# Writing a head's scores in two goes, the second 0.3 slots after the first

## The reference

```python
x = layernorm(x)
q, k, v = proj(Wq, bq), proj(Wk, bk), proj(Wv, bv)          # 16 heads of 16
logits = einsum('bhqd,bhkd->bhqk', q, k) + einsum('bhqd,qkd->bhqk', q, rk)   # rk = embK[clip(k - q, -64, 64) + 64]
w = softmax(logits, axis=-1)
out = einsum('bhqk,bhkd->bhqd', w, v) + einsum('bhqk,qkd->bhqd', w, rv)
```

## Time and profile before

| | |
|---|---|
| median of three runs | 2844.34 us |
| the profiled execution's own time | 2847.89 us |
| its span, first to last instruction | 2846.1 us |
| TensorE busy | 2648.1 us, 93% |
| VectorE busy | 2036.7 us, 72% |
| ScalarE busy | 1573.9 us, 55% |
| GpSimd busy | 1018.2 us, 36% |
| mean granted TensorE clock | 0.983 of full speed |

### The profile page before, as it was taken

One profiled execution on the slowest core, in us unless ns is written; L12 is line 12 of the kernel. 1 busy time (PEld: TensorE's weight loads), 2 busy tenths in 40 slices (PEclk: granted clock), 3 DMA queues, 4 the chain that ended last, 5 costly groups with the idle time before them and its releaser, 6 DMA issues.

```text
span 2846.1 us, 102506 instructions
## 1 busy us (share of the span) xinstructions
PE 2648.1 (93%) x43218; PEld 1971.7 (69%) x43218; DVE 2036.7 (72%) x5187; ACT 1573.9 (55%) x2993; POOL 1018.2 (36%) x2275
## 2 busy tenths in 40 slices
PE   5899999999999999999999999999999999999995
PEld 3567777677776777667776777767777677777773
DVE  4776678676786677866787667776677766787774
ACT  3555556455555555555555565545665455565651
POOL 4113333433334333443234442334323433331025
PEclk8899999999999999999999999999999999999997
DMA  8545644446455464555545556446554456445410
GB/s 224 180 127 169 181 140 129 133 144 181 130 149 145 136 169 131 138 153 160 163 118 144 166 148 162 118 122 175 162 147 126 111 173 180 142 127 145 133 43 27
DMA packets 602999, 409.08 MB, mean 144 GB/s; under 512 B 145578, under 2 KB 602282, under 8 KB 602282
## 3 DMA queue, kind: packets, MB, share of 16 engines
q1 hardware_dynamic: 602538, 402.52, 50.1%
HBM read 206.83 MB, written 194.90 MB: 141 GB/s over the span
## 4 chain that ended last, share of the span: by engine, by line
PE 68%; DVE 16%; issue 5%; ACT 4%; POOL 3%; DMA 0%; SPq 0%; DVEq 0%; ACTq 0%; POOLq 0%
PE logitsT L755 14%; PE oacc L793 14%; PE scores L732 14%; PE logitsT L760 6%; DVE maxes L1012 6%; DVE junk L1009 5%; PE misc L856 4%; PE misc L692 4%; PE misc L818 3%; ACT wxr L1212 2%; PE misc L830 2%; PE misc L706 2%; PE misc L806 2%; POOL rs L1245 1%; DVE stats L915 1%
## 5 line engine op out<-in xcount | busy, mean ns | idle before, releaser
L1009 DVE CUSTOM_DVE_ANT_1 junk<-scores,bands 128x512 bf16<-128x512 f32 x988 | 680.2, 688 | 606.7 <-PE scores L732 588.5
L755 PE MATMUL logitsT<-qs,ks 98*128 98x128 bf16 (+3 forms) x9088 | 995.9, 216 | 33.6 <-ACT wxr L1212 24.6
L1212 ACT ACTIVATE wxr<-logitsT 128x512 f32<-128x512 f32 x1024 | 600.8, 602 | 584.6 <-PE logitsT L755 487.8
L755 PEld LDWEIGHTS logitsT<-qs,ks 98*128 98x128 bf16 (+1 forms) x9088 | 679.6, 99 | 272.4 <-issue 101.3
L1212 ACT ACTIVATE wy<-logitsT 128x512 f32<-128x512 f32 x1024 | 586.3, 596 | 432.1 <-PE logitsT L755 422.4
L732 PE MATMUL scores<-ks,qs 101*128 101x256 bf16 (+10 forms) x4096 | 719.3, 291 | 77.0 <-DVE maxes L1012 39.4
L1012 DVE TENSOR_REDUCE maxes<-scores 128x1 f32<-128x512 f32 x1024 | 701.6, 685 | 2.2 <-PE scores L732 2.2
L732 PEld LDWEIGHTS scores<-ks,qs 96*128 96x128 bf16 (+3 forms) x4096 | 299.7, 100 | 263.0 <-DVE maxes L1012 121.3
L760 PE MATMUL logitsT<-ident,bands 128*128 128x128 f32 x2048 | 468.5, 281 | 0.0
L1240 POOL TENSOR_SCALAR rs<-rs 128x1 int32<-128x1 int32 (+1 forms) x224 | 48.3, 216 | 977.8 <-DVE rs L920 975.3
L760 PEld LDWEIGHTS logitsT<-ident,bands 128*128 128x128 f32 x2048 | 292.7, 143 | 32.9
(11 more groups left out here) (136 smaller groups left out, 2678.8 us busy)
## 6 DMA issues: line engine op xcount, KB each, us to landing
bs<-praw SPq DMA_DIRECT2D x256, 512.0 KB, 4.2
bands<-bs SPq DMA_DIRECT2D x224, 512.0 KB, 4.4
ks<-kd SPq DMA_DIRECT2D x64, 384.0 KB, 4.9
qs<-qd SPq DMA_DIRECT2D x112, 192.0 KB
bands<-bs SPq DMA_DIRECT2D x128, 128.0 KB, 3.4
qd<-qparts SPq DMA_DIRECT2D x64, 192.0 KB, 2.8
kd<-kparts SPq DMA_DIRECT2D x64, 192.0 KB, 2.5
qd<-qparts SPq DMA_DIRECT2D x64, 128.0 KB, 2.6
```

Of the source, the lines that this page charges most:

```text
L755: mm = e.matmul(lt[:, c * P + q0:c * P + q1], kk[0:depth, h, kt * P:(kt + 1) * P], qs[i][0:depth, h, q0:q1], start=q0 == 0, stop=not near, ...
L1009: e.tensor_tensor_reduce(junk[:], scores[:, 0:512].rearrange("p (a c) -> p a c", a=2), banded, 1.0, LOWEST, ALU.add, ALU.max, mx[:, h, 0:1 ...
L1212: e.activation(dst, src, ACT.Exp).then_inc(exp_ready, 1)
```

## The change

The stage `row_max` of a head becomes two stages, `row_max` with half 0 and with half 1. The first keeps its slot, `m0 + 0.87 h`; the second is at `m0 + 0.87 h + 0.3`. On TensorE half 0 writes the first bank and half 1 the second; on VectorE half 0 is the custom instruction with the relative term, half 1 the plain reduction. Each of the two waits for what it waited for before: half 0 of head h+1 for VectorE's half 0 of head h, half 1 of head h+1 for VectorE's half 1 of head h. The instructions are the same in kind, shape and number. Stages whose slots fall between the two places now stand between the two halves, on TensorE and on VectorE. The lists of ScalarE, GpSimd and SyncE are the same as before.

```diff
--- before.py
+++ after.py
@@ -148,7 +148,8 @@
             at(r0 - 15 + 3.5 * blk, "band_write", s, blk)
             at(r0 - 9 + 4 * blk, "band_read", s, blk)
         for h in range(HG):
-            at(m0 + 0.87 * h, "row_max", s, h)
+            at(m0 + 0.87 * h, "row_max", s, h, 0)
+            at(m0 + 0.87 * h + 0.3, "row_max", s, h, 1)
         at(m0 + 6.4, "max_reduce", s)
         at(m0 + 7.4, "max_rows", s)
         at(m0 + 7.45, "max_move", s)
@@ -717,22 +718,21 @@
                                       start=True, stop=True)
                     mm.then_inc(raw_summed, 1)
                 elif stage == "row_max":
-                    s, h = k
+                    s, h, half = k
                     m_, t = s // T, tile_of(s)
                     i, kk = s % QRING, ks[m_ % 2]
-                    u = n("scored", "row_max", s, h) - 1
+                    u = n("scored", "row_max", s, h, half) - 1
                     pe.wait_ge(qs_in[i], q_loads(s))
                     pe.wait_ge(k_ones_in, 32)
-                    pieces = score_pieces(t)
+                    pe.wait_ge(row_maxed, u - 1)
+                    pieces = [x for x in score_pieces(t) if x[0] // 512 == half]
                     for x, (c, key, length, r0, r1, right) in enumerate(pieces):
                         for chunk in range(key // CT, (key + length - 1) // CT + 1):
                             pe.wait_ge(ks_in[m_ % 2][chunk], 16 * (m_ // 2 + 1))
-                        pe.wait_ge(row_maxed, 2 * u - 1 if c < 512 else 2 * u)
                         depth = ROWS if right else SPLIT
                         mm = e.matmul(scores[r0:r1, c:c + length], qs[i][0:depth, h, r0:r1], kk[0:depth, h, key:key + length],
                                       start=True, stop=True, skip_group_check=True)
-                        if x == len(pieces) - 1 or pieces[x + 1][0] // 512 != c // 512:
-                            mm.then_inc(scored, 1)
+                    mm.then_inc(scored, 1)
                 elif stage == "max_rows":
                     s, = k
                     pe.wait_ge(negmax_ready, n("negmax_ready", "max_reduce", s))
@@ -994,25 +994,26 @@
                             .broadcast_to([P, CHUNK, HG, D]), ALU.add)
                     op.then_inc(v_ready, 1)
                 elif stage == "row_max":
-                    s, h = k
+                    s, h, half = k
                     mx = maxes[s % 2]
                     dve.wait_ge(k_ones_in, 32)
-                    u = n("scored", "row_max", s, h) - 1
-                    dve.wait_ge(scored, 2 * u + 1)
+                    u = n("scored", "row_max", s, h, half) - 1
+                    dve.wait_ge(scored, u + 1)
+                    if half:
+                        e.tensor_reduce(mx[:, h, 1:2], scores[:, 512:S], AX.X, ALU.max).then_inc(row_maxed, 1)
+                        continue
                     v = 2 * s + h // HB
                     dve.wait_ge(band_in[v % BRING], band_loads(v))
                     if s >= 2:
                         dve.wait_ge(negmax_ready, s - 1)
-                    dve.wait_ge(row_maxed, 2 * u)
+                    dve.wait_ge(row_maxed, u)
                     at_ = (v % BRING * HB + h % HB) * WIN
                     banded = bass.AP(bands, at_, [[(BRING * HB + 1) * WIN, P], [BRING * HB * WIN - at_, 2], [1, WIN]])
                     e.tensor_tensor_reduce(junk[:], scores[:, 0:512].rearrange("p (a c) -> p a c", a=2), banded, 1.0, LOWEST,
                                            ALU.add, ALU.max, mx[:, h, 0:1]).then_inc(row_maxed, 1)
-                    dve.wait_ge(scored, 2 * u + 2)
-                    e.tensor_reduce(mx[:, h, 1:2], scores[:, 512:S], AX.X, ALU.max).then_inc(row_maxed, 1)
                 elif stage == "max_reduce":
                     s, = k
-                    dve.wait_ge(row_maxed, 2 * n("scored", "row_max", s, HG - 1))
+                    dve.wait_ge(row_maxed, n("scored", "row_max", s, HG - 1, 1))
                     if s >= 2:
                         dve.wait_ge(nm_turned, s - 1)
                     e.tensor_reduce(negmax[s % 2][:], maxes[s % 2][:], AX.X, ALU.max, negate=True).then_inc(negmax_ready, 1)
```

## The result

The changed kernel takes 2870.83 us (median of 4 runs, 2868.95 to 2872.55) against 2844.49 us before (4 runs): the ratio is 1.0089, 95% interval 1.0075 to 1.0103. It is slower by 26 us where 45 us less was forecast, and outside the range.

The account below looks back on a forecast made before the run. TensorE was taken to bound the kernel, held up in places by VectorE. Covered stalls -64, VectorE-bound stretches +7, VectorE's order +12 gave -45: 2844.3 - 45 = 2799, stated as 2800; range 2785 to 2825.

Parts of the forecast that it names:

- What bounds the kernel, and the size of the stalls: TensorE bounds the kernel; its stalls for VectorE's second reduction cost 99 us together, between bounds of 39.4 and 121.3.
- Nothing is added in instructions: Scores keep 4096 matmuls and loads, VectorE its two instructions per head; only the order on these two engines moves.
- Loads come out into the open: On TensorE, the second half's weight load shows behind a short matmul: 37 us, ending at 2840; chance 0.10, shared.
- Second, VectorE's order: ... I take 12: On VectorE, work between a head's reductions delays the second in 254 heads; 12 us given back, ScalarE's exponentials included.
- Third ... They have no wait of their own there that isn't counted.: On TensorE, `weights`, `weighted` and others now run before the second half, without any uncounted wait; nothing added to the sum.
- The slower one, VectorE as hostage of its second half: VectorE idles before its second reduction, delaying queued work and stalling TensorE: 2880, 97 us if all 254 stall; chance 0.14.
- The wait moves: Stalls leave the second bank, return at the first bank, `logitsT` or `relative_sum`: 2838 to 2848; in part, 0.10 shared.

Follow-up runs that it names:

- the five-head kernel: Kernel before, with scores divided on TensorE only at five heads of a quad, none in tile 0, VectorE in the old order: 2832.12 us, 0.9951.
- the last experiment: Kernel before plus 512 small zero matmuls: cutting runs of `weighted`, 2942.16 us (1.0345); as control behind logits blocks, 2854.33 us (1.0034).

## Why the prediction was wrong

**What bounds the kernel, and the size of the stalls.** This held: VectorE's second reduction did stall TensorE for some 97 us, and in the five-head kernel covering part of it made the kernel faster.

**The step that failed first** is "Nothing is added in instructions", with the cost of a break set to nothing. The prediction looked at the break between the halves only as a question of a hidden weight load, in the rival "Loads come out into the open", and drew its evidence from matmuls that all use the whole array. It is a question of how the array is divided. When TensorE goes from matmuls on all columns to matmuls on a part of them, or back, it pays: 0.25 us for one cut [the last experiment]. The second half, put between other work, makes such cuts at two kinds of places: on tile 0, whose own score matmuls are on half of the columns, 22 us; and in the runs of `relative`, 79 cuts, whose price was not measured by itself (at 0.19 to 0.25 us each an estimate of 15 to 20 us). The rule stands in the Trainium skill, page "TensorEngine Tiling (Array Packing)", section "Key Properties": changing the tiling mode drains TensorE. The traces agree in that each change costs time, about 0.25 us for out and back, and don't show by what it is lost; the rule was not weighed.

The price was to be read in the trace of before. After a logits matmul its like starts 0.056 us later, the first fp32 matmul of `weighted` on a 32-column strip 0.149 us, and the first score matmul of tile 0, bf16 on 64 columns, also 0.149 us. On the way back it is 0.205 us from the last strip, where inside the run the next strips come after 0.088, and 0.312 us from the last 512-column matmul on 64 columns, where one on all columns takes 0.216 (all medians of starts). So in and out cost 0.09 and 0.12 us with 32 columns, 0.09 and 0.10 with 64; with 64 no experiment measured it alone. Even a row that the prediction used holds it: the X block of 0.55 us stands in front of `relative`, and one in front of matmuls on all columns lasts 0.47 (1463.18 to 1463.65):

```profile
1463.18 0.22 PE L755 MATMUL logitsT<-qs,ks 98*128 98x128 bf16 x1
...
1463.65 0.60 PE L732 MATMUL scores<-ks,qs 96*128 96x256 bf16 x4
```

A cut run of `relative` in the changed kernel's timeline:

```profile
1456.55 0.49 PE L806 MATMUL misc<-wxr,reltab 128*32 128x64 f32 x16
1457.02 0.39 PE L733 MATMUL scores<-ks,qs 101*128 101x384 bf16 x2
1457.35 0.49 PE L806 MATMUL misc<-wxr,reltab 128*32 128x64 f32 x16
1457.77 0.44 PE L843 MATMUL misc<-ident,attn 128*128 128x128 f32 x2
```

Two pieces in one run took 0.72 us. Here the first takes 0.47 until the second half starts, the second half with its way back 0.33 instead of 0.22, the second piece 0.42: 0.28 us more than 0.72 + 0.22.

**"Second, VectorE's order: ... I take 12".** The mechanism was named, its size was not: the kernel with TensorE's list of before shows 25 us. With TensorE's new list there is no such term: there VectorE's list of before was 7 us slower, so the two orders can't be priced apart. The mean distance of 2.62 us between heads was no measure where what has its slot between the reductions stands just where heads are close. One such place in the changed kernel, first VectorE, then TensorE:

```profile
1452.81 0.67 DVE L1012 CUSTOM_DVE_ANT_1 junk<-scores,bands 128x512 bf16<-128x512 f32 x1
...
1453.42 0.41 DVE L915 BATCH_NORM_STATS2 stats<-x 128x6 f32<-128x256 f32 x1
1453.86 0.18 DVE L918 BATCH_NORM_AGGREGATE mv<-stats 128x2 f32<-128x6 f32 x1
1454.08 0.15 DVE L920 TENSOR_SCALAR rs<-mv 128x1 f32<-128x1 f32 x1
1454.15 0.68 DVE L1003 TENSOR_REDUCE maxes<-scores 128x1 f32<-128x512 f32 x1
```

```profile
1453.55 0.39 PE L733 MATMUL scores<-ks,qs 96*128 96x256 bf16 x2 [0.23 <-DVE maxes L1012]
1454.89 0.39 PE L733 MATMUL scores<-ks,qs 101*128 101x384 bf16 x2 [0.95 <-DVE maxes L1003]
```

The three norm instructions between the reductions take 0.73 us (1453.42 to 1454.15), and the second half of the next head, which has nothing in front of it to cover the wait, starts at 1454.89 instead of 1453.77: 1.1 us lost, where the stall in the earlier trace rows was 0.38. With VectorE's list of before the wait fell to 47.1 us, but the gain went into others, as above: what one list gains hangs on the other.

**"Third ... They have no wait of their own there that isn't counted."** This failed as well. A second half in front of an instruction that waits for another engine was itself the cover of that wait. At head 7 of the second step, `relative_sum` now stands ahead of it:

```profile
1464.74 0.40 PE L733 MATMUL scores<-ks,qs 96*128 96x256 bf16 x2 [0.18 <-DVE maxes L1012]
...
1465.32 0.28 PE L755 MATMUL logitsT<-qs,ks 101*128 101x128 bf16 x2
1465.93 1.31 PE L818 MATMUL misc<-relout,relsel 128*32 128x128 f32 x32 [0.34 <-DVE relout L1044]
1467.17 0.40 PE L733 MATMUL scores<-ks,qs 101*128 101x384 bf16 x2
```

It waits 0.34 us for VectorE's copy, and the second half behind it then costs its 0.22 us in full. By place, against the kernel before, that is 4.5 us here, 4.2 at head 1 of the third step (`out_norm` waits) and 4.2 at head 0 of the second (logits wait for ScalarE).

**The rivals.** The slower one, VectorE as hostage of its second half, has its mark in the trace (143.6 us of VectorE waiting between the reductions) and ended on the right side, but it decides nothing like its 97 us; in the kernel without VectorE's new order that wait is even larger, 168.1 us. One place shows its price: head 1 of the second step loses 7.0 us, as much with VectorE's list of before (6.9) and nothing with TensorE's. There, in the changed kernel, VectorE waits 0.64 us for the second half of the last head of the step before (its reduction starts at 1448.68), and with what is queued behind it comes to head 0 1.59 us after its first score matmul, where it was 0.87. "The wait moves" describes the 105 other steps well: 34.7 us of load wait gone from the second bank in the whole run, nothing in the time of these steps. Its sum was off a little: for 2838 to 2848 it needs give-backs of 58 to 68 us, not 54 to 64.

**The sum as it was.** Tile 0 costs 22 us, and on the other tiles all is balanced: the covered stalls against cut runs (15 to 20, an estimate), VectorE's order and lost covers. How much each of these is was not measured apart. 2845 + 22 = 2867, against 2871 measured.

## What to carry to other kernels

Before moving a group of matmuls between others, look at how each neighbour divides the array: a piece put into a run of another division cost 0.12 to 0.28 us each time here, with no wait row to tell of it. Look for rare shapes too, since one tile in eight made the whole loss. And work that stands in front of a waiting instruction may be what hides that wait: a stall is worth covering only with something that is ready, and place by place, not by a mean.

## What the runs showed of the hardware

A matmul over the whole array inside a run of matmuls on 32-column strips costs 0.19 us of the kernel's time (0.25 on the spot), and 0.02 us between others over the whole array, at a granted clock of 1.00 (2.4 GHz) in most stretches of the run and in those of the timelines here. The 64-column score matmuls lost 0.12 to 0.27 us per divided head, 0.17 in the mean. A change between bf16 and fp32 on all columns cost nothing that the starts show. A granted clock played no part: its mean is 0.98 to 0.99 in every kernel here.
